# First step's layer-1 aggregation: three bf16 parts against the f16 matrix, or two rounded 32 bit parts against a wide copy of it

## The chip, the cores and the metric

The kernel runs on one core of a Trainium2 chip. The metric is device time of one execution in microseconds (us), lower is better. The core has five engines that run their own instruction streams and meet through semaphores: TensorE (PE, matmuls, with its weight loads listed apart as PEld), VectorE (DVE), ScalarE (ACT), GpSimd (POOL) and the queue of SyncE (SP), which starts most DMAs.

## What is computed

The reference runs four graph layers over a batch of 8 graphs with 1024 nodes and 128 features, each followed by a residual sum and a layer norm:

```python
x = _layernorm(x + attention(x, Wq, bq, Wk, Wv, bv))      # softmax over 1024 keys
# layer 1: mean over neighbours, then a linear map and a leaky relu
norm_adj = adj_mat / adj_mat.sum(axis=-1, keepdims=True)
agg = einsum('bnm,bmf->bnf', norm_adj, node_mat)
out = einsum('bnf,of->bno', agg, W) + b
x = _layernorm(x + where(out >= 0, out, 0.01 * out))
x = _layernorm(x + graph_attention(x, adj, W2, a))        # 4 heads, masked softmax
x = _layernorm(x + (D^-1/2 (adj + I) D^-1/2 x) @ B)       # layer 3
```

`adj` holds zeros and ones only, so it is exact in any of the types below. `x` is 32 bit float, and its products with `adj` are wanted at close to that precision.

## The kernel before, in words

Each graph's 1024 nodes lie as 8 tiles of 128 rows. The adjacency is kept as f16 in `adjs[p]` and, transposed by DMA, in `adjTs[p]` (p is the graph's parity). The program is one list of steps: a "first" step, in which graph 0 goes through attention and layer 1; seven "full" steps, in which graph n does that while graph n-1 does layers 2 and 3; and a "last" step for layers 2 and 3 of graph 7. Each engine has its instructions written out in this order, and runs them in it; only semaphores hold them to each other.

Names for what follows:

- `scores` (L1148, L1150) and `context` (L1172) are the attention matmuls on PE. ACT's `exp_tile` (L613) is the softmax numerator.
- On DVE, `context` (L774) makes the attention's output into `x1`, `norm_stats` (L783) and `norm_apply` (L790) are the layer norm, with the root on POOL (L435, L438).
- `split_x1`, by `split_half` (L798 to L804), cuts `x1` into three bf16 parts `parts1`, since the f16/bf16 matmul keeps too few bits of a 32 bit value. It works on halves of four tiles each, and the semaphore `split1` counts four operations of each half.
- PE's `layer1` (L1237) waits for the first half's split, for `y_made[0]` (both halves of the attention's output written) and for the transposed adjacency (`turned`), and calls `aggregate`: 16 pairs of node tile and column half, with three matmuls each of 128x128 weights (a part of `x1`) against 128x512 of `adjT`: 48 in all at L1220, summed up in `Z`. In the first step they run in the order first halves, second halves of `x1`, so that the wait for the second split (`second_half`) comes after 24 of them. Behind the 45th, `times_weights` (L1234) multiplies the first 512 aggregated columns by the layer's weights, behind the 48th the others.
- ACT's `take_sums` (L564) moves the sums from `Z` to `agg1T` between the two. DVE's `layer1_out` (L876 to L881) makes layer 1's output from the result.
- ACT's `make_maskb` (L558) makes the next graph's additive mask `maskb` from `adjs`, one 128x1024 tile an instruction, with the row sums beside it. In the first step the fourth tile comes behind the last `exp_tile`, the other four behind that.
- `cmat` (32 KB of each partition) holds the step matrices of layer 2, `vparts` the three parts of that layer's values. Both are first written in the second step.

Of the kernel before, what the change touches and what calls it, by code (L numbers as in the profile page):

```python
# [35 lines left out]

F32 = mybir.dt.float32
F16 = mybir.dt.float16
BF16 = mybir.dt.bfloat16
ALU = mybir.AluOpType  # L40
ACT = mybir.ActivationFunctionType
AX_X = mybir.AxisListType.X

P = 128
# [29 lines left out]
def gnn_kernel(nc, x, adj, Wq, bq, Wk, WvT, bv, W1T, b1, W2, a2, B3, out):  # L74
    NB, N, D = x.shape
    T = N // P
# [9 lines left out]
    out_v = out.rearrange("b (t p) d -> b p t d", p=P)  # L86
    sj_dram = nc.dram_tensor("sj_rows", (H, N), F32).ap()

# [40 lines left out]
    with ctx:  # L129
        def sb(name, shape, dt):  # L130
            return ctx.enter_context(nc.sbuf_tensor(name, shape, dt))

        def sem(name):
            return ctx.enter_context(nc.semaphore(name))


        adjs = [sb(f"adj{p}", [P, T, N], F16) for p in range(2)]
        adjTs = [sb(f"adjT{p}", [P, T, N], F16) for p in range(2)]
        maskb = sb("maskb", [P, T, N], F16)
        cmat = sb("cmat", [P, 2, T, N], F16)  # L140
        C_OF = [cmat[:, 0, :, :], cmat[:, 1, :, :], maskb[:, :, :], cmat[:, 0, :, :]]

# [2 lines left out]
        def values_in(buffer):  # L145

            return buffer.rearrange("p t n -> p (t n)")[:, 0:2 * T * H * VW].bitcast(F32)\
                .rearrange("p (t h c) -> p t h c", h=H, c=VW)

        VALS = {"full": values_in(cmat[:, 1, :, :]), "last": values_in(adjs[NB % 2][:, :, :])}  # L150
        probs = sb("probs", [P, 2, 2, 512], F32)
        msum = probs[:, :, :, :].rearrange("p a b c -> p (a b c)")[:, 0:T * H * HW]\
            .rearrange("p (t c) -> p t c", t=T)
        x0 = sb("x0", [P, T, D], F32)
        x1 = sb("x1", [P, T, D], F32)
        x2 = sb("x2", [P, T, D], F32)
        x3 = sb("x3", [P, T, D], F32)
        parts1 = sb("parts1", [P, 3, T, D], BF16)
        xT = sb("xT", [P, N], F32)
        qT = sb("qT", [P, N], F32)  # L160
        x2T = sb("x2T", [P, N], F32)
        agg1T, agg3T = qT, x2T
        vparts = sb("vparts", [P, T, H, 3, VW], BF16)
        flat = vparts[:, :, :, :, :].rearrange("p t h s c -> p (t h s c)")
        flat1 = parts1[:, :, :, :].rearrange("p s t d -> p (s t d)")
# [14 lines left out]
        identf = sb("identf", [P, P], F32)  # L180
        ident16 = sb("ident16", [P, P], F16)
        wq_s = sb("wq_s", [P, D], F32)
# [3 lines left out]
        w1_s = sb("w1_s", [P, D], F32)  # L186
# [39 lines left out]
        turned = [sem(f"adj_turned{p}") for p in range(2)]  # L226
# [32 lines left out]
        normed = [sem(f"normed{n}") for n in range(4)]  # L259
        split1 = sem("split1")  # L260
# [21 lines left out]
        rgat_made = sem("rgat_made")  # L282
        gat_made = sem("gat_made")
        diag_added = sem("diag_added")

        block = ctx.enter_context(nc.Block())

# [241 lines left out]
        def _(act):  # L529
# [8 lines left out]
            def sum_row(t):  # L538
                if t >= STEPS:
                    act.wait_ge(rowsums, t - STEPS + 1)  # L540
                act.activation(steps[:, t % STEPS, :], adjs[0][:, t, :], ACT.Copy, bias=-NEG, scale=NEG,
                               accum_out=rowacc[0][:, t:t + 1]).then_inc(rowsums, 1)
# [5 lines left out]
            def make_maskb(g, tiles):  # L548
                for t in tiles:
                    if t % 4 == 0:  # L550

                        act.wait_ge(full["st"], g.before().count(T, t + 4))
                    if t == 0 and (g.base > 1):
                        act.wait_ge(full["c"], g.before().count(2 * H, -2))
                        act.wait_ge(degrees, g.before().count(4))
                    if t % 4 == 0:
                        act.wait_ge(adj_in[g.parity][t // 4], g.count_own(16, 16))
                    act.activation(maskb[:, t, :], adjs[g.parity][:, t, :], ACT.Copy, bias=-NEG, scale=NEG,  # L558
                                   accum_out=rowacc[g.parity][:, t:t + 1]).then_inc(maskb_made, 1)

            def take_sums(name, g, dst, halves=range(2)):
                for c in halves:
                    act.wait_ge(full[name], g.count(2, c + 1))
                    act.activation(dst[:, c * 512:(c + 1) * 512], Z[:, c, :], ACT.Copy).then_inc(read[name], 1)  # L564
# [27 lines left out]
            def factors(o):  # L592
                act.wait_ge(exin_made, o.count(4, 4))
                act.activation(ex[:, :, :, :], exin[:, :, :, :], ACT.Exp).then_inc(ex_made, 1)
# [14 lines left out]
            def exp_tile(kind, g, n):  # L609
                act.wait_ge(full["st"], g.count(T, n + 1))  # L610
                if g.base > 0 or n >= 2:
                    act.wait_ge(probs_used, g.count(T, n - 1))
                act.activation(probs[:, n % 2, :, :], slot(kind, "st", n)[:, :, :], ACT.Exp).then_inc(read["st"], 1)  # L613

            def step(kind, g):
                o = g.before()
                for name, k in {"first": first_opening, "full": opening, "last": heads_up}[kind]:
                    take_group(kind, g, name, k)
                made = 0
                if kind != "last":  # L620
                    for n in range(T):
                        exp_tile(kind, g, n)
                        if kind == "first":
                            if n < 4:
                                sum_row(2 * n)
                                sum_row(2 * n + 1)
                            else:
                                make_maskb(Graph(1), [n - 4])
                        if kind == "full":
                            if n == 0:  # L630
                                factors(o)

                            for n_step in range(made, made + PACE[n]):
                                step_tile(kind, o, n_step)
                            made += PACE[n]
                    if kind == "first":
                        make_maskb(Graph(1), range(4, T))
                if kind != "first":
                    for n in range(made, len(STEP_TILES[kind])):
                        step_tile(kind, o, n)  # L640
                if kind != "last":
                    take_sums("agg1", g, agg1T)
                for c in range(2):
                    if kind == "full" and (g.base < NB - 1):
                        make_maskb(Graph(g.base + 1), range(4 * c, 4 * c + 4))
                    if kind != "first":
                        take_sums("agg3", o, agg3T, [c])

            program(step)


        @block.vector
        def _(dve):
# [140 lines left out]
            def split_half(parts, k, src, done, g, per, at):  # L794
# [8 lines left out]
                dve.wait_ge(done, g.count(per, at + 3))  # L803
                dve.tensor_tensor(parts[:, 2, ts, :], left, parts[:, 1, ts, :], ALU.subtract).then_inc(done, 1)  # L804

            def split_x1(g, k):
                dve.wait_ge(normed[0], g.count(2, k + 1))
                split_half(parts1, k, x1[:, 4 * k:4 * k + 4, :], split1, g, 8, 4 * k)

# [217 lines left out]
        def _(pe):  # L1027
# [181 lines left out]
            def aggregate(kind, g, of, agg, out, parts, mat, second_half, aggT, weights, inside=None):  # L1209

                alone = kind == "last" or (kind == "first" and agg == "agg1")
                for n in range(2 * T):
                    c, t = ((n // 4) % 2, n % 4 + 4 * (n // 8)) if alone else (n // T, n % T)
                    if c == 0 and t == 4:
                        pe.wait_ge(*second_half)
                    for part in range(3):
                        last = pe.matmul(Z[:, c, :], parts[:, part, t, :], mat[:, t, c * 512:(c + 1) * 512],  # L1220
                                         start=t == 0 and part == 0, stop=t == T - 1 and part == 2)
                    if t == T - 1:
                        last.then_inc(full[agg], 1)
                    if c == 0 and t == 1 and inside:
                        inside()
                    if c == 1 and t == (6 if alone else 3):
                        times_weights(kind, g, of, agg, out, aggT, weights, 0)
# [9 lines left out]
            def layer1(kind, g):  # L1237
                pe.wait_ge(split1, g.count(8, 4))
                pe.wait_ge(y_made[0], g.count(2, 2))
                pe.wait_ge(turned[g.parity], g.count_own(16 * T, 16 * T))  # L1240
                aggregate(kind, g, g, "agg1", "out1", parts1, adjTs[g.parity], (split1, g.count(8, 8)), agg1T, w1_s)

            def finish_layer1(kind, g):
                times_weights(kind, g, g, "agg1", "out1", agg1T, w1_s, 1)
# [84 lines left out]
```

## Time and profile before

| | us |
|---|---|
| median of three runs | 987.67 |
| the three runs | 987.3, 990.69, 987.67 |
| the profiled execution | 984.28 |
| its span, first to last instruction | 982.5 |

The profile is of one execution. PE is busy for 875.9 us of the span (89%), DVE for 773.9 us (79%), ACT for 467.5 us (48%), POOL for 355.4 us (36%). A busy PE isn't a PE at its peak: neighbouring matmuls overlap, and the time of one record includes the way through the array, so the pace is read from the start of one to the start of the next. The granted TensorE clock is given as a share of full speed: 1.00 is 2.4 GHz, 0.50 is 1.2 GHz; its mean over the span is 0.978. The stretch of the first step's layer 1 runs from 64 to 80 us.

### The profile page before, as it was taken

Reading aid. Unit: us, or ns where it says so; the run is one execution under the profiler, and the core shown is the slowest. Engines: PE = TensorE matmul, PEld = TensorE weight load, DVE = VectorE, ACT = ScalarE, POOL = GpSimd, SP = SyncE. Lnnn points to the kernel's source line nnn. Section 1 sums busy time; section 2 is a strip of 40 time slices with the busy share of each in tenths; the row PEclk is TensorE's granted clock in tenths of the full one; section 3 lists DMA queues with packets and bytes.
Section 4 is the critical chain, followed back from the end, with each engine's and each line's share of the span. In section 5 each row is a group of like instructions: output and inputs, shape, how many; then the busy total and the mean of one; then the engine's idle time right before and its main releaser. Section 6 shows DMA issues by size and latency. Waiting matters only on the chain.

```text
span 982.5 us, 25692 instructions
## 1 busy us (share of the span) xinstructions
PE 875.9 (89%) x11112; PEld 654.3 (67%) x11112; DVE 773.9 (79%) x1699; ACT 467.5 (48%) x540; POOL 355.4 (36%) x391
## 2 busy tenths in 40 slices
PE   4897999988998989989899899989899898994775
PEld 3564689556985569656795569856697567952772
DVE  2447788788886979878887888878798788885985
ACT  1542573446715575155734467155761557405600
POOL 2021341625224432515316252253325253164612
PEclk9899999999999999999999999999999999997897
DMA  9722110451207220451304502073113512000100
GB/s 183 122 66 43 64 46 4 87 130 29 60 10 138 72 64 26 75 99 45 87 4 86 129 17 72 4 136 79 49 40 67 106 45 65 4 1 22 56 14 22
DMA packets 98881, 60.63 MB, mean 62 GB/s; under 512 B 69040, under 2 KB 86576, under 8 KB 98768
## 3 DMA queue, kind: packets, MB, share of 16 engines
q1 hardware_dynamic: 89280, 41.69, 17.4%
q0 software_dynamic: 8448, 16.78, 9.6%
q8 instruction: 87, 1.43, 0.6%
q10 hardware_dynamic: 1040, 0.52, 0.2%
q14 instruction: 26, 0.21, 0.1%
HBM read 54.66 MB, written 4.33 MB: 60 GB/s over the span
## 4 chain that ended last, share of the span: by engine, by line
PE 69%; DVE 20%; issue 4%; DMA 3%; ACT 3%; POOL 1%; POOLq 0%; DVEq 0%; ACTq 0%
PE ring L1204 19%; PE Z L1220 14%; PE Z L1172 8%; PE ring L1150 8%; PE ring L1185 8%; DVE x L790 6%; DVE cmat L754 4%; DMA adj<-in_adj_dram 3%; PE ring L1234 3%; DVE ring L699 2%; PE ring L1148 2%; PE ring L1088 2%; PE ring L1115 1%; ACT steps L606 1%; DVE meanvar L783 1%
## 5 line engine op out<-in xcount | busy, mean ns | idle before, releaser
L606 ACT ACTIVATE steps<-sjrow,steepsi 128x1024 bf16<-128x1024 f32 x248 | 267.4, 1139 | 123.4 <-DVE cmat L754 92.5
L754 DVE TENSOR_TENSOR cmat<-steps,adj 128x1024 f16<-128x1024 bf16 x180 | 153.8, 898 | 24.5 <-ACT steps L606 22.6
L1204 PE MATMUL ring<-vparts,cmat 128*128 128x66 bf16 x4416 | 143.6, 194 | 18.1 <-DVE cmat L754 12.1
L1172 PEld LDWEIGHTS Z<-vv,probs 128*128 128x128 f32 x1024 | 122.6, 191 | 52.6 <-ACT probs L613 37.3
L1204 PEld LDWEIGHTS ring<-vparts,cmat 128*128 128x128 f16 x4416 | 141.1, 98 | 19.4 <-issue 7.2
L435 POOL TENSOR_SCALAR vareps<-meanvar 128x4 f32<-128x4 f32 x64 | 13.3, 208 | 387.9 <-DVE meanvar L783 387.0
L1172 PE MATMUL Z<-vv,probs 128*128 128x129 f32 x1024 | 126.5, 277 | 25.4 <-ACT probs L613 25.4
L1150 PE MATMUL ring<-qT,xT 128*128 128x512 f32 x256 | 138.9, 624 | 0.0
L613 ACT ACTIVATE probs<-ring 128x1024 f32<-128x1024 f32 x64 | 65.1, 1017 | 68.0 <-PE ring L1150 68.0
L699 DVE CUSTOM_DVE_ANT_0 ring<-ring,maskb 128x1024 f32<-128x1024 f32 x64 | 78.4, 1229 | 21.9 <-PE ring L1088 21.9
L1220 PE MATMUL Z<-adjT,vparts 128*128 128x512 f16 x384 | 88.1, 383 | 7.9 <-DVE vparts L804 7.9
L1185 PE MATMUL ring<-vparts,adj 128*128 128x132 bf16 x1536 | 94.0, 222 | 0.1
L1185 PEld LDWEIGHTS ring<-vparts,adj 128*128 128x128 f16 x1536 | 93.3, 96 | 0.3 <-issue 0.2
L1220 PE MATMUL Z<-adjT,parts 128*128 128x512 f16 x384 | 85.6, 379 | 1.9 <-DVE x L774 1.6
L564 ACT ACTIVATE qT<-Z 128x512 f32<-128x512 f32 x16 | 9.6, 597 | 156.4 <-PE Z L1220 156.4
L790 DVE TENSOR_SCALAR x<-x,meanvar,rstd 128x128 f32<-128x128 f32 x192 | 77.0, 467 | 4.4 <-POOL rstd L438 4.4
L438 POOL TENSOR_TENSOR rstd<-vareps,powers 128x4 f32<-128x4 f32 x64 | 71.6, 1119 | 5.3
L1220 PEld LDWEIGHTS Z<-adjT,vparts 128*128 128x128 bf16 x384 | 37.9, 99 | 50.8 <-DVE vparts L804 8.0
L1148 PEld LDWEIGHTS ring<-ident,maskb 128*128 128x128 f16 x512 | 39.1, 99 | 43.8 <-issue 41.2
L1220 PEld LDWEIGHTS Z<-adjT,parts 128*128 128x128 bf16 x384 | 37.0, 98 | 44.0 <-issue 1.8
L558 ACT ACTIVATE maskb<-adj 128x1024 f16<-128x1024 f16 x56 | 58.4, 1044 | 13.1 <-DMA adj<-in_adj_dram 13.0
L1088 PE MATMUL ring<-parts 128*128 128x512 bf16 x128 | 39.5, 395 | 16.7 <-DVE parts L960 9.5
(126 smaller groups left out, 1300.3 us busy)
## 6 DMA issues: line engine op xcount, KB each, us to landing
adj<-in_adj_dram POOLq DMA_DIRECT2D x16, 1024.0 KB, 12.4
sjrow<-sj_rows SPq DMA_DIRECT2D x31, 512.0 KB, 3.9
out_dram<-x SPq DMA_DIRECT2D x16, 256.0 KB, 2.4
x<-in_x_dram SPq DMA_DIRECT2D x7, 512.0 KB, 4.3
adjT<-adj SPq DMA_TRANSPOSE x64, 3.4
x<-in_x_dram ACTq DMA_DIRECT2D x1, 512.0 KB, 4.5
sjbuf<-in_a_dram SPq DMA_DIRECT2D x1, 128.0 KB, 11.1
sj_rows<-sjbuf SPq DMA_DIRECT2D x8, 16.0 KB
```

Source lines behind the costliest of these rows:

```text
L438: pool.tensor_tensor(rstd[:, layer, ts], vareps[:, layer, ts], powers[:, 0:4, 0], ALU.pow)\
L606: act.activation(steps[:, n % STEPS, :], sjrow[:, h % 2, :], ACT.Relu, bias=steepsi[:, t, h:h + 1], scale=STEEP).then_inc(step_made, 1)
L613: act.activation(probs[:, n % 2, :, :], slot(kind, "st", n)[:, :, :], ACT.Exp).then_inc(read["st"], 1)
L699: dve.tensor_tensor_reduce(out=s, in0=s, in1=maskb[:, t, :], scale=1.0, scalar=LOWEST, op0=ALU.add, op1=ALU.max, accum_out=smax[:, t:t + 1 ...
L754: dve.tensor_tensor(c_of[:, t, :], steps[:, n % STEPS, :], adjs[o.parity][:, t, :], ALU.min)\
L790: ins = dve.tensor_scalar(xn[:, t, :], xn[:, t, :], meanvar[:, layer, t, 1:2], rstd[:, layer, t:t + 1], ALU.subtract, ALU.mult)
L1088: last = pe.matmul(s[:, c, :], qb[:, t * P:(t + 1) * P], xb[:, c * 512:(c + 1) * 512], start=True, stop=True)
L1150: last = pe.matmul(s[:, j, :], xT[:, kt * P:(kt + 1) * P], qT[:, c * 512:(c + 1) * 512], start=False, stop=True, skip_group_check=True)
L1172: last = pe.matmul(zq[:, q, 0:D + 1], probs[:, n % 2, j, q * P:(q + 1) * P], vv[:, kt, :], start=kt == 0 and q % 2 == 0, stop=kt == T - 1, ...
L1185: last = pe.matmul(s[:, j, 0:H * HW], adjs[o.parity][:, t, jt * P:(jt + 1) * P], vparts[:, t, :, part, HW:VW], start=t == 0 and part == 0, ...
L1204: last = pe.matmul(s[:, jt, 0:VW], c_of[:, t, jt * P:(jt + 1) * P], vparts[:, t, h, part, :], start=t == 0 and part == 0, stop=t == T - 1 ...
L1220: last = pe.matmul(Z[:, c, :], parts[:, part, t, :], mat[:, t, c * 512:(c + 1) * 512], start=t == 0 and part == 0, stop=t == T - 1 and par ...
```

## The change

It touches the first step alone. A 32 bit type that keeps fewer bits of a float (`float32r`, the "rounded" one) takes the place of bf16 and f16 in graph 0's layer 1. Two tensors are laid into room that is used later only: `wideT` (128 x 8 x 1024, where `cmat` is) and `wide1` (two parts of `x1`, where `vparts` is).

- ACT copies `adjTs[0]` to `wideT`, eight instructions of 128x1024, between the last `exp_tile`'s mask tile and the remaining four mask tiles.
- DVE's `split_wide` makes two parts of each half of `x1` by two operations in place of four.
- PE issues 32 matmuls in place of 48, and waits for all eight copies (`widened`) before the first.

```diff
+        with nc.sbuf_tensor("wideT", [P, T, N], F32R) as wideT:
+            pass
         cmat = sb("cmat", [P, 2, T, N], F16)
...
+        with nc.sbuf_tensor("wide1", [P, 2, T, D], F32R) as wide1:
+            pass
         vparts = sb("vparts", [P, T, H, 3, VW], BF16)
...
                     if kind == "first":
+                        act.wait_ge(turned[0], 16 * T)
+                        for t in range(T):
+                            act.activation(wideT[:, t, :], adjTs[0][:, t, :], ACT.Copy).then_inc(widened, 1)
                         make_maskb(Graph(1), range(4, T))
...
+            def split_wide(k):
+
+                ts = slice(4 * k, 4 * k + 4)
+                dve.wait_ge(normed[0], k + 1)
+                dve.tensor_copy(wide1[:, 0, ts, :], x1[:, ts, :]).then_inc(split1, 2)
+                dve.wait_ge(split1, 4 * k + 2)
+                dve.tensor_tensor(wide1[:, 1, ts, :], x1[:, ts, :], wide1[:, 0, ts, :].bitcast(F32), ALU.subtract).then_inc(split1, 2)
+
             def split_x1(g, k):
+                if g.base == 0:
+                    split_wide(k)
+                    return
...
-                    for part in range(3):
+                    number = 2 if kind == "first" else 3
+                    for part in range(number):
                         last = pe.matmul(Z[:, c, :], parts[:, part, t, :], mat[:, t, c * 512:(c + 1) * 512],
-                                         start=t == 0 and part == 0, stop=t == T - 1 and part == 2)
+                                         start=t == 0 and part == 0, stop=t == T - 1 and part == number - 1)
...
                 pe.wait_ge(turned[g.parity], g.count_own(16 * T, 16 * T))
-                aggregate(kind, g, g, "agg1", "out1", parts1, adjTs[g.parity], (split1, g.count(8, 8)), agg1T, w1_s)
+                if kind == "first":
+                    pe.wait_ge(widened, T)
+                    aggregate(kind, g, g, "agg1", "out1", wide1, wideT, (split1, g.count(8, 8)), agg1T, w1_s)
+                else:
+                    aggregate(kind, g, g, "agg1", "out1", parts1, adjTs[g.parity], (split1, g.count(8, 8)), agg1T, w1_s)
```

On ACT, at the end of the first step, the order before is (`probs` is the exponential's tile, `maskb` the next graph's mask, `qT` the room of the aggregated sums):

```order
L613 ACTIVATE probs<-ring 128x1024 [waits probs_used,st_full]
L558 ACTIVATE maskb,rowacc<-adj 128x1024
L558 ACTIVATE maskb,rowacc<-adj 128x1024 [waits adj_in1_half1,st_full]
L558 ACTIVATE maskb,rowacc<-adj 128x1024 x3
L564 ACTIVATE qT<-Z 128x512 [waits agg1_full] x2
```

and in the changed kernel, whose line numbers are higher by 7 there:

```order
L620 ACTIVATE probs<-ring 128x1024 [waits probs_used,st_full]
L565 ACTIVATE maskb,rowacc<-adj 128x1024
L646 ACTIVATE wideT<-adjT 128x1024 [waits adj_turned0]
L646 ACTIVATE wideT<-adjT 128x1024 x7
L565 ACTIVATE maskb,rowacc<-adj 128x1024 [waits adj_in1_half1,st_full]
L565 ACTIVATE maskb,rowacc<-adj 128x1024 x3
L571 ACTIVATE qT<-Z 128x512 [waits agg1_full] x2
```

The eight copies stand ahead of four mask tiles and of both moves of the sums.

On PE, the same place in the program runs from the last attention matmuls to graph 1's first transposes (L1059). Before:

```order
L1172 MATMUL Z<-vv,probs 128x129 x7
L1220 MATMUL Z<-adjT,parts 128x512 [waits y_made0,adj_turned0,split1,late_in]
L1220 MATMUL Z<-adjT,parts 128x512 x23
L1220 MATMUL Z<-adjT,parts 128x512 [waits split1]
L1220 MATMUL Z<-adjT,parts 128x512 x20
L1234 MATMUL ring<-w_s,qT 128x128 [waits agg1_read,st_read]
L1234 MATMUL ring<-w_s,qT 128x128 x3
L1220 MATMUL Z<-adjT,parts 128x512 x3
```

and in the changed kernel:

```order
L1193 MATMUL Z<-vv,probs 128x129 x7
L1242 MATMUL Z<-wideT,wide 128x512 [waits adj_turned0,y_made0,widened,split1,late_in]
L1242 MATMUL Z<-wideT,wide 128x512 x15
L1242 MATMUL Z<-wideT,wide 128x512 [waits split1]
L1242 MATMUL Z<-wideT,wide 128x512 x13
L1256 MATMUL ring<-w_s,qT 128x128 [waits agg1_read,st_read]
L1256 MATMUL ring<-w_s,qT 128x128 x3
L1242 MATMUL Z<-wideT,wide 128x512 x2
```

The first matmul waits for `widened` as well, the second half's wait comes after 16 in place of 24, and the weights of layer 1 after 30 in place of 45.

## Rows read from the trace of the kernel before

**Rows 1.** The page: busy time of each engine, share of the span, instructions.

```profile
PE 875.9 (89%) x11112; PEld 654.3 (67%) x11112; DVE 773.9 (79%) x1699; ACT 467.5 (48%) x540; POOL 355.4 (36%) x391
```

**Rows 2.** Chain that ended last, 60 to 91 us: start, us, engine, what.

```profile
60.37 3.59 PE Z L1172 x32
...
64.20 1.14 DVE x L774 x4
...
67.68 1.13 DVE x L790 x4
...
68.83 0.44 DVE parts L798
...
70.48 0.70 DVE parts L804
...
71.23 4.71 PE Z L1220 x21
75.93 0.91 PE ring L1234 x8
...
76.86 1.14 DVE x L876 x4
...
85.13 3.13 DVE x L790 x4
...
89.61 1.01 PE ring L1088 x2
```

**Rows 3.** Timeline of ACT: start, us, line, operation [idle before <-releaser].

```profile
60.41 1.02 ACT L613 ACTIVATE probs<-ring 128x1024 f32<-128x1024 f32 x1 [2.00 <-PE ring L1150]
...
62.36 1.04 ACT L558 ACTIVATE maskb<-adj 128x1024 f16<-128x1024 f16 x1
63.31 0.19 ACT L558 ACTIVATION_READ_ACCUMULATOR maskb<-adj 128x1 f32 x1
...
65.48 1.04 ACT L558 ACTIVATE maskb<-adj 128x1024 f16<-128x1024 f16 x1
...
74.03 0.60 ACT L564 ACTIVATE qT<-Z 128x512 f32<-128x512 f32 x1 [7.41 <-PE Z L1220]
```

**Rows 4.** Windows: us, each engine's busy us, granted clock (PEclk), DMA share, GB/s.

```profile
20.00:23.00 3.00, 0.00 (x0) 0.00 (x0) 2.40 (x5) 0.00 (x0) 0.00 (x0) 0.70 1.11 201
40.00:60.00 20.00, 20.00 (x141) 14.91 (x140) 8.77 (x26) 12.04 (x19) 1.24 (x2) 1.00 0.00 1
...
85.00:89.00 4.00, 0.20 (x2) 0.01 (x1) 3.87 (x6) 1.02 (x1) 2.41 (x2) 1.00 0.00 0
89.00:90.00 1.00, 0.39 (x2) 0.14 (x3) 0.47 (x1) 0.00 (x0) 0.00 (x0) 0.74 0.00 0
90.00:92.00 2.00, 2.00 (x10) 1.80 (x9) 1.20 (x2) 0.00 (x0) 0.00 (x0) 0.50 0.00 0
92.00:93.00 1.00, 1.00 (x5) 0.41 (x4) 0.09 (x2) 0.63 (x1) 0.00 (x0) 0.55 0.00 0
```

**Rows 5.** ACT's step tiles (L606): ns min/median/max, first and last start, form.

```profile
L606 ACT ACTIVATE steps<-sjrow,steepsi x248: 1132/1137/1151, 106.2 to 937.9; 128x1024 bf16<-128x1024 f32 x124
```

**Rows 6.** Timeline of PE, the first step's layer 1.

```profile
65.58 5.34 PE L1220 MATMUL Z<-adjT,parts 128*128 128x512 f16 x24 [1.64 <-DVE x L774]
...
75.77 1.05 PE L1234 MATMUL ring<-w_s,qT 128*128 128x128 f32 x8
```

**Rows 7.** The aggregation's weight loads and matmuls, all steps: ns min/median/max.

```profile
L1220 PEld LDWEIGHTS Z<-adjT,parts x384: 95/98/100, 65.6 to 871.8; 128*128 128x128 bf16 x192
L1220 PE MATMUL Z<-adjT,parts x384: 376/379/389, 65.6 to 872.0; 128*128 128x512 f16 x192
```

**Rows 8.** Timeline of two 32 bit matmuls of 512 columns (L1072) and their weight loads.

```profile
81.46 1.96 PE L1072 MATMUL ring<-xT,wqk 128*128 128x512 f32 x4 [1.21 <-DVE x L876]
...
81.97 0.19 PEld L1072 LDWEIGHTS ring<-xT,wqk 128*128 128x128 f32 x1 [0.24 <-issue]
82.39 0.19 PEld L1072 LDWEIGHTS ring<-xT,wqk 128*128 128x128 f32 x1 [0.24 <-issue]
```

More of the change, by code:

```diff
@@ L37 @@
 F32 = mybir.dt.float32
+F32R = mybir.dt.float32r
 F16 = mybir.dt.float16
@@ L284, in gnn_kernel @@
         diag_added = sem("diag_added")
+        widened = sem("widened")
         block = ctx.enter_context(nc.Block())
```

## The prediction

> **What bounds the kernel now.** The page comes first: PE is busy for 89% of the span, DVE for 79%, ACT for only 48% [rows 1]. Shares over a span of 982.5 us say little of a change that touches one stretch of some 12 us, so the next view is the chain of waits there [rows 2]. The reader is to see in it that the end is handed on without a gap from PE's last attention matmuls (until 63.96) to DVE (L774, from 64.20), through the layer norm to DVE's split of the second half of `x1` (68.83 to 71.18), to PE's second batch of aggregation matmuls (71.23), its weights (L1234) and to DVE's `layer1_out`, which starts at 76.86 and is the next thing that everything waits for. From there DVE is on the chain until PE's matmuls of graph 1 at 89.61. So what the change is worth is how much sooner or later than 76.86 the first half of layer 1's output is ready for DVE; the second half isn't late, since DVE has over 3 us of work on the first. What comes later follows from this point in the same order, and I carry the difference to the end one for one.
>
> The first batch of aggregation matmuls starts at 65.58, when DVE's L774 has ended [rows 6], and isn't on the chain: it fills PE's time while the second half is normed and split.
>
> **What goes.** On PE 16 of 48 matmuls. Their pace is (5.34 - 0.38) / 23 = 0.216 us from one start to the next, with 24 in 5.34 us [rows 6] and 0.38 us for one record [rows 7]. Of the 24 removed or moved from the first batch none was on the chain. On DVE two of the four operations of each split go. The second split, on the chain before, should end after one copy and one subtraction, at 68.83 + 0.44 + 0.02 + 0.70 = 69.99 in place of 71.18 [rows 2], 1.2 us sooner; a 32 bit output is costed as the bf16 output of the same 512 elements.
>
> **What is new on ACT, and is late next.** The eight copies stand behind the fourth mask tile and ahead of the other four. ACT is free for them at 62.36, where the next mask tile starts now [rows 3]. The transposes that they read are done: no DMA moved anything between 40 and 60 us [rows 4]. The same-sized mask tile lasts 1.04 us, and the instruction behind it (its accumulator's read) starts 0.95 us after it [rows 3]; a copy has no such read, so I take 0.95 us from start to start. The last copy ends at 62.36 + 7 x 0.95 + 1.04 = 70.05. ACT's slowest form over 1024 elements, the step tile, lasts 1.14 us [rows 5]: eight of those in line give 71.5, the upper end. The lower end is the 0.95 itself: elements and engine are the same, and the output is wider, so I exclude a gain.
>
> PE waits for all eight, so its first aggregation matmul moves from 65.58 to about 70.15 (0.1 us for the semaphore). The second split (69.99) is then ready before 16 matmuls have run, and that wait is hidden. Behind the copies on ACT stand four mask tiles of 1.04 us, which end at about 74.2 in place of 66.5, and then the move of the sums, which waits for PE until later than that; today ACT idles for 7.41 us in front of it [rows 3], and this idle time is the cover. The masks are for graph 1's scores, at 89.6 and after [rows 2]. Both cost nothing.
>
> **PE's matmuls.** No row shows a matmul of the rounded type. The nearest rows bound it. The f16 one of 512 columns takes 0.216 us. The plain 32 bit one comes as two records, spaced by 0.42 us (weight loads at 81.97 and 82.39 [rows 8]), 0.84 us in all. One instruction with one record can then be 0.216 us (the rate of 16 bit) or 0.42 us (the rate of a 32 bit record). I take 0.216: the type gives up bits, and the two records of the plain one look like the price of the full ones. The weight load of 32 bit takes 0.19 us against 0.098 [rows 7, 8]; it is issued while the matmul before it runs [rows 8], and is shorter than 0.216, so I cost it at nothing; uncovered it would cost 0.19 us a matmul.
>
> The Trainium skill, FP8 and Floating Point Precision, section TensorE Precision Notes, says that true 32 bit takes four passes through the array, and that there is a reduced form which reads four bytes and cuts them to about 22 bits. The trace agrees on the first: 0.84 us is 3.9 times 0.216. If the rounded type is that reduced form in one pass, the sum is the one that I take; by the nearest row of its width it would be the second rival below. No run here shows it so far.
>
> **The clock.** PE is now idle from 63.96 to 70.15, 6.2 us. In the trace the granted clock falls from 1.00 to 0.50 in idle stretches of that kind: it averages 0.70 over 20 to 23 us, where PE does nothing, and stands at 0.50 from 90 to 92, after PE's idle time from 85.2 to 89.61, and at 0.55 from 92 to 93 [rows 2, 4]. The matmuls that begin at 89.61 thus run for about 3.3 us (until 92.9) at 1.2 GHz, and work of 3.3 us at half the pace loses 1.65 us. Before the change the idle stretch at this place is 1.6 us and the clock holds. I take 1.65 us; the ends are 0 (it doesn't fall) and 3.5 (all 32 matmuls, 6.9 us at full clock, run at half).
>
> **The sum.** PE starts at 70.15; 30 matmuls are 30 x 0.216 = 6.48; the clock 1.65; from the start of the weights' matmuls to DVE's start 76.86 - 75.77 = 1.09 as now [rows 2, 6]. That is 79.37 in place of 76.86: 2.5 us later. The profiled execution took 984.28 us; it would take 986.8. The median of the runs is 987.67, 3.4 us above the profiled one, so I forecast 987.67 + 2.5 = 990.2 us, with 987.5 to 993.5 as this case's own range (1.4 us for slower copies, 1.65 less or 1.85 more for the clock, and the scatter of a median). A measurement of this kernel tells 0.5%, 4.9 us, from no change; this is inside it.
>
> **Rivals.**
> 1. The clock costs nothing on balance: either it doesn't fall, 990.2 - 1.65 = 988.5, or it falls here and PE's later idle stretch (85.2 to 89.6) no longer makes it fall, so that the half-clock stretch only changes its place, the same 988.5; with both, 986.9. For it: between 89 and 90 us the clock averages 0.74 [rows 4], so it fell only just ahead of that stretch's end, and a small shift could spare it. Against it: 6.2 us of idle time are more than the 4.4 us there.
> 2. The other side, slower: the rounded matmul runs at the rate of a 32 bit record, or each waits for its own 0.19 us weight load. Place: the 30 matmuls ahead of L1234. Price: 30 x (0.42 - 0.216) = 6.1 us, or 5.7 for the weights; the time is 996.3. It decides from 0.216 + (4.9 - 2.5) / 30 = 0.30 us a matmul. For it: each operand has twice the bytes of 16 bit, and the only 32 bit record in this trace has this pace. Against it: the plain 32 bit matmul spends two records on more bits.
> 3. The type doesn't do what its name says, and each matmul goes out as two 32 bit records: 30 x (0.84 - 0.216) = 18.7 us more, 1008.9. Nothing in the trace speaks for it but that all 32 bit matmuls here are so.
> 4. Faster by over 0.5%: even were the copies ready at 65.58, where PE is released now, 65.58 + 6.48 + 1.09 = 73.15 would be 3.7 us sooner, under the bound. It needs a gain elsewhere, which no row offers.
>
> **How the numbers follow.** The forecast has 0.60, rival 1 0.20, rival 2 0.15, rival 3 0.03, rival 4 0.02. Within 0.5% fall the forecast (but for 0.03 of its upper tail) and rival 1: 0.77. Slower by more: rivals 2 and 3 and that tail, 0.21. Faster: rival 4, 0.02. The range runs from rival 1's lower end to rival 2 with the slower copies (996.3 + 1.4): 986.5 to 997.5. It leaves out rival 3, rival 4 and the scatter beyond.
>
> **What would show it.** In the profile after: eight ACT instructions about 0.95 us apart from 62.4 on, the last ending near 70; PE idle from 64 to about 70.1 with `widened` as its releaser; a granted clock of 0.50 in the first microseconds of the aggregation; 32 records of it, 0.216 us apart once the clock is back at 1.00; DVE's two-operation split ending near 70.0 with nobody waiting for it; `layer1_out` starting near 79.4, and the chain beyond it shifted by the same amount. The forecast is wrong if the records stand 0.42 us apart at full clock, if there are 64 of them, if the copies take longer than 1.14 us each, or if the shift at `layer1_out` doesn't reach the end of the span.

## The result, and the profile after

| | before | after |
|---|---|---|
| median of 20 runs each, us | 987.48 | 990.83 |
| lowest to highest, us | 984.27 to 990.86 | 988.77 to 992.24 |
| profiled execution, us | 984.28 | 990.93 |
| its span, us | 982.5 | 989.1 |
| its mean granted clock | 0.978 | 0.968 |

The ratio is 1.0033, with a 95% interval of 1.0024 to 1.0042: 3.35 us slower, inside the 0.5% of the forecast, which was 990.2 us.

The chain of waits in the changed kernel, at the place of [rows 2] (start, us, engine, what; L897 is `layer1_out`, L1242 the aggregation, L1256 the weights, L800 the norm, L1109 graph 1's first scores):

```profile
68.89 0.44 DVE wide L820
...
69.42 0.70 DVE wide L822
...
70.17 9.90 PE Z L1242 x30
80.07 0.91 PE ring L1256 x8
...
81.00 1.14 DVE x L897 x4
...
89.27 3.13 DVE x L800 x4
...
94.13 0.63 PE ring L1109
```

DVE's `layer1_out` starts at 81.00 in place of 76.86, 4.1 us later. The split of the second half, on the chain before until 71.18, ends at 70.12; but now all 30 matmuls ahead of the weights stand behind that moment, where 21 did. ACT's timeline shows the copies:

```profile
62.36 7.67 ACT L646 ACTIVATE wideT<-adjT 128x1024 fp32r<-128x1024 f16 x8
69.93 1.05 ACT L565 ACTIVATE maskb<-adj 128x1024 f16<-128x1024 f16 x1
...
78.75 0.60 ACT L571 ACTIVATE qT<-Z 128x512 f32<-128x512 f32 x1 [4.57 <-PE Z L1242]
```

They end at 70.03 (forecast 70.05), the mask tiles behind them are done by 74.2, and ACT still idles for 4.57 us ahead of the sums: that cover held. Then PE's timeline, and below it the windows (length, PE's busy us, granted clock, DMA share, GB/s):

```profile
70.17 9.90 PE L1242 MATMUL Z<-wideT,wide 128*128 128x512 f32 x30 [6.24 <-DVE wide L822]
79.91 1.05 PE L1256 MATMUL ring<-w_s,qT 128*128 128x128 f32 x8
```

```profile
64.00:68.00 4.00, 0.00 (x0) 0.75 0.21 57
...
70.00:71.00 1.00, 0.83 (x2) 0.50 1.27 282
...
75.00:76.00 1.00, 1.00 (x4) 0.50 1.09 212
76.00:77.00 1.00, 1.00 (x6) 0.89 0.95 188
77.00:78.00 1.00, 1.00 (x6) 1.00 0.95 181
```

PE is idle for 6.24 us, the clock falls to 0.50 within that time and stays there until about 76.2: 6.0 us of the aggregation at 1.2 GHz, where I had 3.3. The releaser that the first line names, DVE's L822, ended at 70.12, and the last copy at 70.03: two signals within 0.1 us, of which the view takes the later. The program's order speaks for the copies: PE's first matmul waits for the split of the first half alone, and that was done at 56.3; the wait for the second half stands 16 matmuls later.

```profile
55.57 0.69 DVE L822 TENSOR_TENSOR wide<-x,wide 128x512 fp32r<-128x512 f32 x1
```

Experiments 2 and 3 test which one PE waited for.

The profiled executions differ by 6.6 us in span, the medians by 3.35. The rest of the 6.6 lies where the change does nothing. From the chain of the kernel before, the norm ahead of graph 2's first scores and the last step's long matmul groups (L1204 is its sums over the heads, L1220 its aggregation):

```profile
198.14 4.01 DVE x L790 x8
...
934.33 18.13 PE ring L1204 x576
960.36 11.32 PE Z L1220 x45
```

and of the changed kernel, with the load of graph 2's adjacency ahead of it:

```profile
181.62 13.77 DMA adj<-in_adj_dram
...
202.66 4.01 DVE x L800 x8
...
938.82 19.62 PE ring L1225 x576
966.37 11.91 PE Z L1242 x45
```

The shift is 4.0 us when the second step's head inputs start (95.84 before, 99.81 after), 4.5 at that norm, since that one transfer landed last in this execution, and stays 4.5 until 934.33 against 938.82. Behind that the same 576 matmuls take 1.5 us longer and the 45 of the last aggregation 0.6. The granted clock shows it (length, PE's busy us, granted clock, DMA share, GB/s), before

```profile
934.00:938.00 4.00, 3.67 (x119) 1.00 0.19 57
...
962.00:966.00 4.00, 4.00 (x17) 0.84 0.00 0
```

and after:

```profile
938.00:942.00 4.00, 3.18 (x72) 0.72 0.23 70
...
966.00:970.00 4.00, 3.63 (x9) 0.50 0.00 0
```

Both stretches stand behind idle time of PE. Ahead of the 576 matmuls it is 3.28 us before, and the clock holds; it is 2.36 us after, and the clock falls to 0.50 at about 939.9. So the length of an idle stretch alone doesn't tell whether the clock falls. The 576 matmuls take 19.4 to 19.6 us in the profiles of all six experiments too, so the one profile of the kernel before, whose execution is at the low end of its 20 runs, is the odd one. One profile doesn't tell whether that kernel is always spared there; that the medians differ by only 3.35 us speaks against it.

### The profile page after: what moved, and what is told of

Its sections match the earlier page's. It is cut to its first block, busy times and chain, and to the rows that moved or that the text cites. A ratio compares the mean times of both kernels' runs of the same rounds, so it can differ in the third digit from the quotient of the medians.

```text
span 989.1 us, 25653 instructions
## 1 busy us (share of the span) xinstructions
PE 874.6 (88%) x11081; PEld 659.3 (67%) x11096; DVE 771.6 (78%) x1695; ACT 474.9 (48%) x548; POOL 355.4 (36%) x391
## 4 chain that ended last, share of the span: by engine, by line
PE 66%; DVE 20%; DMA 4%; issue 4%; ACT 4%; POOL 1%; POOLq 0%; DVEq 0%; ACTq 0%
PE ring L1225 19%; PE Z L1242 13%; PE Z L1193 8%; PE ring L1171 8%; PE ring L1206 8%; DVE x L800 6%; DMA adj<-in_adj_dram 4%; DVE cmat L764 3%; PE ring L1256 2%; DVE ring L709 2%; PE ring L1169 2%; PE ring L1109 2%; PE ring L1136 1%; ACT steps L613 1%; DVE meanvar L793 1%
## 5 line engine op out<-in xcount | busy, mean ns | idle before, releaser
L1225 PE MATMUL ring<-vparts,cmat 128*128 128x66 bf16 x4416 | 146.3, 195 | 17.1 <-DVE cmat L764 12.1
L1193 PEld LDWEIGHTS Z<-vv,probs 128*128 128x128 f32 x1024 | 122.6, 191 | 52.6 <-ACT probs L620 37.3
L1225 PEld LDWEIGHTS ring<-vparts,cmat 128*128 128x128 f16 x4416 | 143.8, 99 | 18.5 <-issue 7.2
L1193 PE MATMUL Z<-vv,probs 128*128 128x129 f32 x1024 | 126.5, 277 | 25.4 <-ACT probs L620 25.4
L1242 PE MATMUL Z<-adjT,vparts 128*128 128x512 f16 x384 | 88.7, 385 | 7.9 <-DVE vparts L814 7.9
L800 DVE TENSOR_SCALAR x<-x,meanvar,rstd 128x128 f32<-128x128 f32 x192 | 77.0, 467 | 4.4 <-POOL rstd L445 4.4
L1242 PE MATMUL Z<-adjT,parts 128*128 128x512 f16 x336 | 74.8, 379 | 0.0
L1242 PEld LDWEIGHTS Z<-adjT,vparts 128*128 128x128 bf16 x384 | 38.0, 99 | 51.3 <-DVE vparts L814 8.1
L1242 PEld LDWEIGHTS Z<-adjT,parts 128*128 128x128 bf16 x336 | 32.4, 98 | 36.5
L1109 PE MATMUL ring<-parts 128*128 128x512 bf16 x113 | 35.8, 393 | 21.0 <-DVE parts L981 13.5
```

Source lines behind the costliest of these rows:

```text
L800: ins = dve.tensor_scalar(xn[:, t, :], xn[:, t, :], meanvar[:, layer, t, 1:2], rstd[:, layer, t:t + 1], ALU.subtract, ALU.mult)
L1193: last = pe.matmul(zq[:, q, 0:D + 1], probs[:, n % 2, j, q * P:(q + 1) * P], vv[:, kt, :], start=kt == 0 and q % 2 == 0, stop=kt == T - 1, ...
L1225: last = pe.matmul(s[:, jt, 0:VW], c_of[:, t, jt * P:(jt + 1) * P], vparts[:, t, h, part, :], start=t == 0 and part == 0, stop=t == T - 1 ...
```

## The experiments

Six kernels ran. Since attention ends up to 1.6 us earlier or later from one execution to the next, I measure from the start of the last 32 attention matmuls (L1172 before, L1193 after) to the start of `layer1_out`, and set beside it the timed ratio to the kernel before on the same chip.

| kernel | last attention matmuls, us | layer1_out, us | between | against before | ratio of times (95%) |
|---|---|---|---|---|---|
| before | 60.21 | 76.86 | 16.65 | | |
| after | 60.20 | 81.00 | 20.80 | +4.15 | 1.0033 (1.0024 to 1.0042) |
| 1 keep busy | 61.33 | 79.30 | 17.97 | +1.32 | 1.0011 (1.0001 to 1.0021) |
| 2 copies early | 60.76 | 75.15 | 14.39 | -2.26 | 0.9978 (0.9968 to 0.9988) |
| 3 wait alone | 61.75 | 84.26 | 22.51 | +5.86 | 1.0065 (1.0052 to 1.0079) |
| 4 half columns | 60.14 | 78.47 | 18.33 | +1.68 | none (one execution) |
| 5 busy elsewhere | 61.10 | 75.47 | 14.37 | -2.28 | 0.9937 (0.9918 to 0.9957) |
| 6 half busy | 61.49 | 81.00 | 19.51 | +2.86 | 1.0034 (1.0018 to 1.005) |

### 1. PE kept busy through the wait

```diff
+                if kind == "first":
+                    idle = claim(kind, g, "out1", 0)
+                    for _ in range(27):
+                        pe.matmul(idle[:, 0, :], ident16[:, :], adjs[0][:, 0, 0:512], start=True, stop=True)
                 pe.wait_ge(split1, g.count(8, 4))
```

> The changed kernel, with 27 matmuls of 128x512 f16 that nothing reads put on PE between the last attention matmul and the aggregation, into a PSUM room that is free then: 27 x 0.216 = 5.8 us, from 63.95 to about 69.8, so PE is idle for 0.4 us in place of 6.2. Theory A (the clock): the aggregation's 0.43 us spacing from 70.2 to 76 us is the half granted clock after the idle time; here the clock stays at 1.00, all 32 records stand 0.216 us apart, the weights start at about 76.7 and layer1_out at 77.8, 3.2 us sooner than the 81.00 of the changed kernel and still 0.9 later than before. Timed: 1.5 to 3.3 us below the changed kernel's 990.83 (before 987.48), so a ratio to before of 1.000 to 1.002. Rival B (the rounded operands themselves start slowly, for instance since ACT and the DMA queue write while PE reads 4 byte operands): clock 1.00, but the records still 0.43 us apart until about 76, layer1_out at 81 and the time of the changed kernel, ratio 1.0033.

PE's timeline, and the granted clock of two windows in the aggregation:

```profile
64.91 5.99 PE L1263 MATMUL ring<-adj,ident 128*128 128x512 f16 x27
71.30 7.07 PE L1242 MATMUL Z<-wideT,wide 128*128 128x512 f32 x30 [0.41 <-DVE wide L822]
78.21 1.05 PE L1256 MATMUL ring<-w_s,qT 128*128 128x128 f32 x8
```

```profile
70.00:72.00 2.00, 1.59 (x8) 1.00 1.27 241
...
74.00:76.00 2.00, 2.00 (x11) 1.00 1.04 198
```

The clock holds at 1.00, the 30 records take 7.07 us in place of 9.90, and `layer1_out` gains 2.8 us on the changed kernel. Theory A holds, rival B falls: the rounded operands aren't slow by themselves, though the pace stays a little above the 0.216 us that was expected. In time it is 1.0011 against 1.0033 of before, some 2.2 us; the clock's share of the change's loss is thus about two thirds, and 1.1 us stay (0.1 to 2.1 by the interval). A second reading: records are (7.07 - 0.39) / 29 = 0.230 us from start to start (0.39 is one record), while the 27 f16 matmuls just ahead stand (5.99 - 0.38) / 26 = 0.216 apart.

### 2. The copies moved to ACT's idle time

```diff
                             else:
-                                make_maskb(Graph(1), [n - 4])
+                                if n == 4:
+                                    act.wait_ge(turned[0], 16 * T)
+                                for t in (2 * n - 8, 2 * n - 7):
+                                    act.activation(wideT[:, t, :], adjTs[0][:, t, :], ACT.Copy).then_inc(widened, 1)
...
-                        act.wait_ge(turned[0], 16 * T)
-                        for t in range(T):
-                            act.activation(wideT[:, t, :], adjTs[0][:, t, :], ACT.Copy).then_inc(widened, 1)
-                        make_maskb(Graph(1), range(4, T))
+                        make_maskb(Graph(1), range(T))
```

> The changed kernel, with the eight wide copies put two and two behind the last four exponentials of the first step (ACT idles for 1 to 2 us in front of each now), and all eight mask tiles of graph 1 behind the last of them. Theory A (the copies' place on ACT delays PE, and with it comes the clock): the last copy ends at about 63.3, before the attention's output at 65.3; PE starts the aggregation at 65.6 as in the kernel before, at clock 1.00, runs 16 matmuls until 69.0, waits 1.1 us for the second split (70.1), and layer1_out starts at 70.1 + 14 x 0.216 + 1.09 = 74.2, which is 2.7 us sooner than before (76.86) and 6.8 sooner than the changed kernel (81.00). Timed: 2 to 3.5 us below before, ratio 0.9965 to 0.998. Rival C (it isn't the copies that release PE but the second split by DVE, as the profile names it; they ended within 0.1 us of each other): PE starts at 70.1 here too, and nothing is gained over the changed kernel but perhaps the clock. Rival D (the copies delay the exponentials): the attention ends later by up to 4 x 0.3 us, and the gain is that much smaller.

ACT's first and last pair of copies, and below them PE:

```profile
49.70 1.99 ACT L638 ACTIVATE wideT<-adjT 128x1024 fp32r<-128x1024 f16 x2
52.84 1.02 ACT L620 ACTIVATE probs<-ring 128x1024 f32<-128x1024 f32 x1 [1.15 <-PE ring L1171]
...
61.88 1.99 ACT L638 ACTIVATE wideT<-adjT 128x1024 fp32r<-128x1024 f16 x2
```

```profile
66.09 3.88 PE L1242 MATMUL Z<-wideT,wide 128*128 128x512 f32 x16 [1.60 <-issue]
70.74 3.48 PE L1242 MATMUL Z<-wideT,wide 128*128 128x512 f32 x14 [0.77 <-DVE wide L822]
```

ACT still idles for 1.15 us ahead of each exponential between the copies, so rival D falls. PE starts after 1.60 us of idle time, as before, runs 16 matmuls while DVE norms the second half, and waits for the split in the middle. Rival C falls: the first batch needs only the copies and the first half. The way to `layer1_out` is 2.26 us shorter than before and 6.4 shorter than in the changed kernel; in time 0.9978, 2.2 us below before. The same matmuls and the same copies are thus a loss or a gain by the copies' place (the four mask tiles that stood there went behind the last exponential). Against [rows 2] the gain has two parts: the split ends earlier, by about 1.0 us against the attention's end, and 14 matmuls stand behind it in 3.48 us in place of 21 in 4.71.

### 3. The copies and the wait, with the matmuls of before

```diff
-                    aggregate(kind, g, g, "agg1", "out1", wide1, wideT, (split1, g.count(8, 8)), agg1T, w1_s)
+                    aggregate(kind, g, g, "agg1", "out1", parts1, adjTs[0], (split1, g.count(8, 8)), agg1T, w1_s)
...
-                    number = 2 if kind == "first" else 3
+                    number = 3
...
-                if g.base == 0:
-                    split_wide(k)
-                    return
```

> The eight copies and PE's wait for them are kept, and nothing reads the copies: DVE's split into three bf16 parts and the 48 f16 matmuls are those of the kernel before. It measures the price of the wait without the saving in matmuls. Theory A: PE starts at 70.15, the second split ends at 71.2 and is hidden, the clock is at 0.50 for 3 to 6 us (1.6 to 3 us lost), the weights start after 45 matmuls at 70.15 + 9.72 + 1.6 to 3 = 81.5 to 82.9 and layer1_out at 82.6 to 84.0, that is 5.7 to 7.1 us later than before, and the timed difference is the same size, ratio 1.005 to 1.0075, as the shift goes to the end one for one. Rival E (a shift at this place is taken up later, by waits for DMA or by DVE's slack): layer1_out is late by 6 to 7 us, but the time only by the 3 us of the changed kernel or less.

The chain, and PE's windows behind it:

```profile
64.01 7.58 ACT wideT L646 x8
...
71.72 11.61 PE Z L1239 x45
83.33 0.91 PE ring L1253 x8
...
84.26 1.14 DVE x L894 x4
```

```profile
72.00:74.00 2.00, 2.00 (x6) 0.50 1.16 234
74.00:76.00 2.00, 2.00 (x8) 0.68 1.00 195
76.00:78.00 2.00, 2.00 (x11) 1.00 1.02 192
```

DVE's longer split of the second half ends only at 72.7 here, behind PE's start, so it can't be taken for the releaser; the chain names ACT's copies, of which the last ends at 71.58. The shift is 5.86 us at `layer1_out` and 6.2 in time (1.0065): theory A, and rival E falls, since a shift here reaches the end whole. The copies' wait costs about 6 us with 48 matmuls and 3.3 with 32, so the saved matmuls (with the cheaper split) give back somewhat under 3 us.

### 4. What a rounded matmul costs

On the kernel of experiment 1, each rounded matmul cut into two of 256 columns:

```diff
+                        if kind == "first":
+                            for w in range(2):
+                                at = slice(c * 512 + w * 256, c * 512 + (w + 1) * 256)
+                                last = pe.matmul(Z[:, c, w * 256:(w + 1) * 256], parts[:, part, t, :], mat[:, t, at],
...
```

> The kernel of e1_keep_busy, whose rounded matmuls stood 0.230 us apart at full clock where the f16 ones stand 0.216 apart, with each of the 32 cut into two of 256 columns (64 matmuls, the same products, weights loaded twice as often). It asks what sets the 0.230. Theory F (the weight load of 32 bit, 0.19 us of record against 0.098, is nearly as long as the 512 columns): the 256-column matmuls stand about 0.19 to 0.23 us apart, the 60 ahead of the weights take 11.4 to 13.8 us in place of 6.9, and layer1_out is 4.5 to 6.9 us later than in e1_keep_busy after the attention's end. Theory G (the rounded matmul costs its columns and a small fixed part): they stand 0.115 us apart, and nothing else moves by more than 0.5 us.

PE's timeline, then its weight loads and matmuls (ns min/median/max):

```profile
70.12 7.42 PE L1245 MATMUL Z<-wideT,wide 128*128 128x256 f32 x60 [0.41 <-DVE wide L822]
```

```profile
L1245 PEld LDWEIGHTS Z<-wideT,wide x64: 186/192/192, 70.1 to 78.5; 128*128 128x128 f32 x64
L1245 PE MATMUL Z<-wideT,wide x64: 278/283/363, 70.1 to 78.6; 128*128 128x256 f32 x64
```

The records are (7.42 - 0.28) / 59 = 0.121 us apart, though each loads its weights in 0.19 us: theory G (it expected 0.115). 64 loads of 0.19 us would be 12 us in a row, so they overlap, and the load isn't the bound. From 256 to 512 columns the pace grows by 0.109 us, which leaves about 0.012 us of a fixed part. This is one profile of one execution, so its time says nothing more.

### 5. PE kept busy in two other idle stretches

On the kernel of experiment 2:

```diff
+            def busy(room, times):
+                for _ in range(times):
+                    pe.matmul(room[:, 0, :], ident16[:, :], adjs[1][:, 0, 0:512], start=True, stop=True)
...
+                if t == 0 and g.base == 1:
+                    busy(s, 19)
...
+                if kind == "last":
+                    busy(claim(kind, g, "out3", 0), 34)
```

> The kernel of e2_copies_early (ratio to before 0.9978), with matmuls that nothing reads put into two idle stretches of PE that the change doesn't touch: 19 (4.1 us) behind graph 1's value projection, where PE waits for DVE from 85.2 to 89.6 in the kernel before, and 34 (7.3 us) ahead of the last step's aggregation, where it waits for DVE from 952.5 to 960.3. Theory A (what idle time costs is the granted clock of the work behind it): the clock stays at 1.00 behind both, the aggregation's 45 records in the last step take 9.8 us in place of 11.3 to 12.1, graph 1's first scores gain about 1.5 us, and the time falls by 2 to 4 us below e2_copies_early's 985.5, ratio to before 0.994 to 0.996. Rival H (DVE bounds both places, so PE's pace behind them is hidden): the clock stays up and the time stays within 1 us of e2_copies_early's, ratio 0.997 to 0.999.

PE's timeline in the last step:

```profile
950.73 7.50 PE L1105 MATMUL ring<-adj,ident 128*128 128x512 f16 x34
958.81 9.89 PE L1248 MATMUL Z<-adjT,vparts 128*128 128x512 f16 x45 [0.58 <-DVE vparts L814]
```

and the same place of experiment 2's kernel:

```profile
960.49 11.51 PE L1242 MATMUL Z<-adjT,vparts 128*128 128x512 f16 x45 [7.91 <-DVE vparts L814]
```

The 45 matmuls take 9.89 us in place of 11.51, and at the first place the chain is 1.7 us shorter (from the last attention matmuls of the first step to the head inputs at L1136 or L1142, 32.9 us in place of 34.6). The granted clock is 1.00 from 82 to 93 us and from 935 to 975 us, where experiment 2's kernel has 0.50 from 88 to 93 and a mean of 0.62 from 960 to 965. In time the kernel is at 981.66 us, ratio 0.9937, a little more than theory A's 0.994 to 0.996, and faster than both kernels of this case; rival H falls. Its six runs lie within 1.1 us (981.16 to 982.21), the 17 of the kernel before on that chip within 5.8 (984.64 to 990.41). That would fit a scatter that comes from where the clock falls, but it isn't shown: the four runs of experiment 3, whose clock does fall, lie within 0.4 us.

### 6. Half of the idle time filled

Experiment 1 with 13 in place of 27 matmuls.

> The kernel of e1_keep_busy with 13 in place of 27 idle matmuls, so that PE is idle for about 3.4 us ahead of the aggregation: between the 1.6 us of the kernel before, where the clock held, and the 6.2 us of the changed kernel, where it fell to 0.50 until 76.1. If 3.4 us aren't enough for the clock to fall: e1_keep_busy's layer1_out, about 18.0 us behind the start of the last attention matmuls, and its time (988.6). If they are: 19.5 to 21 us behind it and 990 to 991 us.

PE's timeline, and its windows:

```profile
71.46 8.61 PE L1242 MATMUL Z<-wideT,wide 128*128 128x512 f32 x30 [3.43 <-DVE wide L822]
```

```profile
70.00:72.00 2.00, 0.54 (x1) 0.84 1.29 264
72.00:74.00 2.00, 2.00 (x6) 0.50 1.10 216
74.00:76.00 2.00, 2.00 (x8) 0.81 1.05 195
76.00:78.00 2.00, 2.00 (x10) 1.00 0.97 186
```

Idle for 3.43 us, PE still finds the clock at 0.50, from about the moment at which it starts again until about 74.8. In the kernel before, 1.64 us of idle time left it at 1.00:

```profile
64.00:65.50 1.50, 0.00 (x0) 1.00 0.00 0
```

`layer1_out` is 1.5 us later than in experiment 1, and the time is that of the changed kernel (1.0034, 1.0018 to 1.005). In the profile `layer1_out` is 1.3 us sooner than in the changed kernel; the timing, with an interval of 1.6 us to either side, doesn't show that gain.

## Why the prediction was right

The mechanism is the one that was forecast: PE waits for the copies, its clock falls meanwhile, and the shift goes to the end. In the profile the terms add up to 70.17 + 30 x 0.230 + 2.8 + 1.09 = 81.0 for `layer1_out`, where I had 79.37: 1.6 us later, of which the clock is 1.2 and the pace 0.4. The medians moved by only 3.35 us, against the 2.5 of the forecast, and the median that I added to was 0.2 us high. That the time came within 0.6 us of 990.2 is thus partly luck.

**The wait (right).** The copies were forecast to end at 70.05 and PE to start at 70.15; the trace has 70.03 and 70.17. That the copies release PE can't be read from the view of the changed kernel, since the other signal came within 0.1 us; experiment 3 names the copies, and experiment 2, where they are early, lets PE start 4.6 us sooner, counted from the last attention matmuls.

**The matmuls (right in kind, too cheap by 6%).** One record each, at the pace of 16 bit: 0.230 us where I put 0.216. Over 30 of them that is 0.4 us, which with the rest of experiment 1 makes +1.3 us in place of my +0.86 without the clock. The second and third rival are out: no 0.42 us at full clock, no second record. The Trainium skill (FP8 and Floating Point Precision, TensorE Precision Notes) names a reduced form of 32 bit that is cut to about 22 bits, and gives neither its passes nor its time. The pace here fits one pass; that the rounded type is that form no run shows.

**The clock (right in kind, too small).** This is the term that was mis-sized: 1.65 us forecast, 2.8 in the profile (experiment 1 against the changed kernel) and about 2.2 in the medians. I took the 3.3 us of half clock seen at 89.6; here 6.0 us of matmuls ran at it in the profiled execution, 3.6 in experiment 3 and 3.3 in experiment 6, so one row was too little to size it by. Rival 1 (no cost on balance) is out: PE's later idle stretch makes the clock fall in the changed kernel as it did before (0.50 from 94 to 96 us).

**The covers (right).** Mask tiles and the second split cost nothing. ACT idles ahead of the sums, and no wait of PE stands in the middle of its 30 matmuls.

**One for one to the end (right).** In the profiles `layer1_out` is late by 4.15, 1.32, -2.26, 5.86 and 2.86 us (after, experiments 1 to 3 and 6), and the medians differ from before by 3.35, 0.92, -2.18, 6.25 and 3.54: the same within 0.8 us. The profiled pair's 6.6 us overstates it, mostly by its last step.

**Two sums.** Rival 4's bound, 73.15, left out that the last 14 matmuls wait for the second split. Experiment 2 has the copies ready in time: 14.39 us from the last attention matmuls to `layer1_out`, where that bound is 12.94. The ends of the whole range should be 986.9 and 997.7 by their terms, not 986.5 and 997.5; nothing hangs on it.

What stays open: why the clock falls at one idle stretch and not at another, why the half-clock stretch was longer in one execution than in another, and why graph 2's adjacency load landed 0.5 us late in the profile after (the norm behind it starts 102.85 us after the second step's head inputs there, 102.3 before and in experiments 1, 5 and 6). None of these was tried.

## What to carry to other kernels

A cheaper type for one engine's operands is paid by the engine that converts them, and what counts is where that engine stands when it has to: with the same eight copies the change lost 3.3 us when they stood behind the last exponential, and gained 2.2 us when they stood in the idle time between the last four. Count a new wait of the matmul engine twice, once for itself and once for the granted clock of the work behind it. Where idle time can't be avoided, matmuls that nothing reads are worth a try, over the whole stretch: half of it gave nothing that the timing could show.

## What the runs showed of the hardware

- A rounded 32 bit matmul is one record and runs at 0.230 us for 512 columns (experiment 1) and 0.121 for 256 (experiment 4), where f16 takes 0.216 for 512, though its weight load of 0.19 us is twice that of 16 bit. The plain 32 bit matmul takes two records of 0.42 us [rows 8].
- Two idle stretches of 5.0 and 7.9 us in a kernel whose PE is busy for 89% of the span cost some 3.5 us of it, by the clock of the work behind them (medians of experiments 2 and 5 are 2.18 and 5.64 us below their own runs of the kernel before; the profiles show 1.7 and 1.6 us at the two places).
- An idle stretch of 3.28 us left the clock at 1.00 in one profile, and one of 2.36 us at the same place was followed by 0.50 in another. How long the half clock then lasted differed as well: 3.3 to 6.0 us of matmuls in the first step's aggregation.
